# Third attention of a four-layer network: first key and value products split into context and own tokens, part of them moved ahead of the norms

## What is computed

```python
# second feed-forward part, on layernorm(x)
qg, sg = dynamic_quant(x, inv_gate); qu, su = dynamic_quant(x, inv_up)
inter = clip(silu(quant_gemm(qg, sg, w_gate)) * quant_gemm(qu, su, w_up))
x = x + tanh(g) * quant_gemm(*dynamic_quant(inter, inv_inter), w_down)

# third attention, latents = layernorm(x), 32 heads of 128, 4 key/value heads
hidden = concatenate([context, latents], axis=1)      # 64 + 64 tokens per batch
q = latents @ Wq
k, v = hidden @ Wk, hidden @ Wv                       # 4 key/value heads
attn = softmax(q @ k.T / sqrt(128))
x = x + tanh(g) * ((attn @ v) @ Wo)
```

## Time and profile before

| | us |
|---|---|
| median of 3 runs (1638.70 to 1640.34) | 1639.47 |
| the profiled execution's own time | 1636.33 |
| its span, first to last instruction | 1634.5 |
| TensorE busy | 1533.6 (94%) |
| VectorE, ScalarE, GpSimd busy | 905.2, 698.4, 637.8 |
| mean granted TensorE clock | 0.982 of full |

### The profile page before, as it was taken

The page is one execution under the profiler, slowest core; times in us unless marked ns, Lnnn a source line. Parts: engine busy times, 40 slices in busy tenths (PEclk is TensorE's granted clock), DMA queues, the critical chain, the costliest instruction groups (busy, mean ns, idle before and its releaser), DMA issues.

```text
span 1634.5 us, 25536 instructions
## 1 busy us (share of the span) xinstructions
PE 1533.6 (94%) x8786; PEld 1219.5 (75%) x8786; DVE 905.2 (55%) x1805; ACT 698.4 (43%) x2005; POOL 637.8 (39%) x606
## 2 busy tenths in 40 slices
PE   7898989888699999999999998899899999999998
PEld 6666766577588888888888887777677777777776
DVE  7887778768602212222221234687766776676666
ACT  5443244445335435443544445452434343433432
POOL 4643444655413313231322133343644544454430
PEclk9999999899899999999999999899999999999999
DMA  5101110031201000110101011123312212112101
GB/s 213 40 1 39 46 39 1 1 113 46 85 32 40 27 26 27 40 52 2 52 1 52 1 52 58 40 80 83 108 40 78 65 53 73 58 54 76 30 14 53
DMA packets 27885, 81.41 MB, mean 50 GB/s; under 512 B 3248, under 2 KB 11952, under 8 KB 22768
## 3 DMA queue, kind: packets, MB, share of 16 engines
q1 hardware_dynamic: 26896, 79.44, 14.7%
q10 hardware_dynamic: 864, 0.30, 0.1%
HBM read 69.25 MB, written 10.49 MB: 49 GB/s over the span
## 4 chain that ended last, share of the span: by engine, by line
PE 53%; issue 12%; DVE 4%; POOL 3%; ACT 1%; POOLq 0%; DVEq 0%; ACTq 0%
PE bank L397 33%; PE bank L1391 7%; PE bank L1379 2%; PE pair L2453 2%; PE bank L2431 2%; PE pair L1360 2%; POOL wo_low L388 1%; PE pair L397 1%; PE bank L1368 1%; POOL wq_low L1116 1%; PE bank L2439 1%; POOL probs L1125 1%; DVE probs L2285 0%; DVE out_low L2315 0%; DVE small L222 0%
## 5 line engine op out<-in xcount | busy, mean ns | idle before, releaser
L1301 DVE SCALAR_TENSOR_TENSOR x_stream<-bank,gates,x_stream 128x512 f32<-128x512 f32 x64 | 48.1, 751 | 352.3 <-PE bank L1391 352.3
L397 PE MATMUL bank<-hid_high,wq_high 128*128 128x512 f32 (+1 forms) x576 | 234.6, 407 | 1.7 <-issue 1.5
L397 PE MATMUL bank<-hid_high,wq_low 128*128 128x512 f32 (+1 forms) x576 | 220.2, 382 | 0.0
L397 PE MATMUL bank<-hid_low,wq_high 128*128 128x512 f32 (+1 forms) x576 | 218.6, 380 | 0.1
L1125 POOL TENSOR_TENSOR probs<-probs,small 128x512 f32<-128x512 f32 x64 | 67.0, 1048 | 357.5 <-DVE small L1289 357.5
L2180 ACT ACTIVATE probs<-probs,small 128x64 f32<-128x64 f32 x256 | 86.1, 338 | 133.7 <-DVE small L2304 133.7
L397 PEld LDWEIGHTS bank<-hid_high,wq_high 128*128 128x128 f32 x576 | 108.8, 189 | 24.1 <-issue 3.1
L1199 ACT ACTIVATE probs<-pair,small 128x128 f32<-128x128 f32 x256 | 90.5, 366 | 82.6 <-DVE small L1283 82.6
L397 PEld LDWEIGHTS bank<-hid_high,wq_low 128*128 128x128 f32 x576 | 108.7, 189 | 22.6
L397 PEld LDWEIGHTS bank<-hid_low,wq_high 128*128 128x128 f32 x576 | 109.2, 190 | 19.3 <-issue 2.0
L608 POOL TENSOR_TENSOR probs<-probs,small 128x512 f32<-128x512 f32 x64 | 67.2, 1049 | 112.0 <-DVE small L830 111.6
(11 more groups left out here) (382 smaller groups left out, 4185.4 us busy)
## 6 DMA issues: line engine op xcount, KB each, us to landing
raw_q<-in_L_wq SPq DMA_DIRECT2D x18, 1024.0 KB, 4.9
raw_o<-in_L_wo SPq DMA_DIRECT2D x18, 1024.0 KB, 4.9
values<-ctx_values SPq DMA_DIRECT2D x32, 256.0 KB, 3.9
values_t<-ctx_keys SPq DMA_DIRECT2D x8, 512.0 KB, 3.3
raw_c<-in_L_wkv SPq DMA_DIRECT2D x6, 512.0 KB, 3.4
raw_o<-in_L_wkv SPq DMA_DIRECT2D x5, 512.0 KB, 4.6
x_stream<-in_x SPq DMA_DIRECT2D x8, 256.0 KB, 10.7
ctx_keys<-raw_o SPq DMA_DIRECT2D x8, 256.0 KB, 2.0
```

What stands on the lines that cost most here:

```text
L397: last = k.nc.tensor.matmul(out, stationary(a, c), moving(b, c), start=n == 0, stop=n == total - 1)
L1301: nc.vector.scalar_tensor_tensor(xt, k.bank[7][:], gate, xt, ALU.mult, ALU.add).then_inc(k.x_done, 1)
```

## The change

Six things change; what is computed does not.

1. The six products are split by tokens: `wide_context_half(k, e, side)` makes a product over the context tokens (side 0) or the own ones (side 1), 12 matmuls with 256 columns (4 batches by 64 tokens), written with a stride into one half of each batch's columns of the bank. The bank is complete when both have run.
2. The six banks are 0, 1, 4, 5, 6, 7, one per product, and ScalarE evicts each from there.
3. The context halves of e = 0 and 1 run at the end of the integer layer, after `down(7)` and ahead of the barrier; that of e = 2 ahead of the first transposes, those of 3, 4 and 5 between the transposes. The own halves come by group m, once tiles 2m and 2m+1 are in `hid_low`.
4. The split of the first key and value weights moves into slot 11 of the integer layer: the cast on ScalarE ahead of that slot's other work, the subtraction on GpSimd behind the update of tile 6.
5. The three powers of `next_rstd_gpsimd` move from the end of the integer layer into its slots 8, 10 and 12, each ahead of that slot's update.
6. VectorE's norms go by pairs of tiles (apply two, low of the two before), and ScalarE evicts the products between the `hid_high` copies; the four `high_q` come after tile 3.

```diff
+FIRST_BANKS = (0, 1, 4, 5, 6, 7)
+def wide_context_half(k, e, side):
+    m, kv = divmod(e, 2)
+    out = k.bank[FIRST_BANKS[e]][:].rearrange("p (b s n) -> p b s n", b=4, s=2)[:, :, side, :]
+    return product(k, out, lambda s, c: k.wc[s][:, kv * D + c * P:kv * D + (c + 1) * P],
+                   lambda part, c: hid_cols(k, part, c, 4 * m, 4, side), C)
...
@@ attention_middle, gpsimd
-        low_c(0)
         for head in range(4):
             low_q(0, 0, head)
@@ attention_middle, scalar
-        high_c(0)
-        for t in range(T):
+        for t in range(4):
             ln_high_scalar(k, act, t)
-            if t == 2:
-                for head in range(4):
-                    high_q(0, 0, head)
-        for e in range(6):
-            context(0, e)
-            if e in (3, 5):
-                value_back(0, e // 2 - 1, 13 + 2 * (e // 2 - 1))
+        for head in range(4):
+            high_q(0, 0, head)
+        for m in range(3):
+            for e in (2 * m, 2 * m + 1):
+                context(0, e, FIRST_BANKS[e])
+                if m == 2:
+                    value_back(0, e - 4, 13 + 2 * (e - 4))
+            for t in (2 * m + 4, 2 * m + 5):
+                if t < T:
+                    ln_high_scalar(k, act, t)
@@ attention_middle, vector
-        prep_vector(k, dve)
+        for p in range(T // 2 + 1):
+            if p < T // 2:
+                for t in (2 * p, 2 * p + 1):
+                    ln_apply_vector(k, dve, t)
+            if p == 0:
+                last_stats_vector(k, dve)
+            else:
+                for t in (2 * p - 2, 2 * p - 1):
+                    ln_low_vector(k, dve, t)
@@ attention_middle, tensor
-        for t in range(T):
-            ln_transpose_tensor(k, pe, t, k.xn_ready)
-            if t in (3, 5):
-                if t == 3:
-                    pe.wait_ge(k.lo_c, k.at("lo_c", 2))
-                pe.wait_ge(k.xt_lo, k.at("xt_lo", 2))
-                context(0, t // 2 - 1)
-        pe.wait_ge(k.xt_lo, k.at("xt_lo", T))
-        for e in range(2, 6):
-            pe.wait_ge(k.kv_sbuf, k.at("kv_sbuf", e - 1))
-            context(0, e)
-            if e in (3, 5):
-                m = e // 2 - 1
-                values_back(0, m, 13 + 2 * m)
+        def own_tokens(m):
+            pe.wait_ge(k.xt_lo, k.at("xt_lo", 2 * m + 2))
+            for e in (2 * m, 2 * m + 1):
+                wide_context_half(k, e, 1).then_inc(k.kv_psum, 1)
+                if m == 2:
+                    pe.wait_ge(k.xt_lo, k.at("xt_lo", T))
+                    values_back(0, e - 4, 13 + 2 * (e - 4))
+        wide_context_half(k, 2, 0)
+        for p in range(T // 2):
+            for t in (2 * p, 2 * p + 1):
+                ln_transpose_tensor(k, pe, t, k.xn_ready)
+            if p < 2:
+                wide_context_half(k, 3 + p, 0)
+            if p == 1:
+                own_tokens(0)
+                wide_context_half(k, 5, 0)
+            if p >= 2:
+                own_tokens(p - 1)
@@ quant_mlp, gpsimd
+            if s in (8, 10, 12):
+                ln_rstd_gpsimd(k, pool, s // 2 - 4, s // 2 - 2)
             if s >= 5:
                 update(s - 5)
-        next_rstd_gpsimd(k, pool)
+            if s == 11:
+                split_low_gpsimd(k, pool, k.raw_c, k.wc, 1024, k.hi_c, k.at("hi_c", 0), k.lo_c)
@@ quant_mlp, scalar
+            if s == 11:
+                act.wait_ge(k.loaded_c, k.at("loaded_c", 32))
+                act.wait_ge(k.s_psum, k.at("s_psum", T))
+                split_high_scalar(k, act, k.raw_c, k.wc, 1024, k.hi_c)
@@ quant_mlp, tensor
+        pe.wait_ge(k.x_scaled, k.at("x_scaled", T))
+        for e in range(2):
+            pe.wait_ge(k.lo_c, k.at("lo_c", e + 1))
+            wide_context_half(k, e, 0)
```

More of the change, by code:

```diff
@@ L1168, in high_o, with context @@
             split_high_scalar(k, act, k.raw_o, k.wo, 2048, k.hi_o)
-        def context(j, e):
+        def context(j, e, bank=None):
             m = e // 2
@@ L1179, in context @@
                 dst = VT[:, m % 2]
-            nc.scalar.copy(dst, k.bank[4 + e % 2][:]).then_inc(k.kv_sbuf, 1)
+            bank = k.bank[4 + e % 2 if bank is None else bank]
+            nc.scalar.copy(dst, bank[:]).then_inc(k.kv_sbuf, 1)
         def value_back(j, m, s):
```

## The result

| | before | changed |
|---|---|---|
| median, same chip, 4 runs each | 1639.90 | 1627.47 (1626.05 to 1628.89) |
| ratio of the runs, 95% interval | | 0.9928 [0.9916, 0.9940] |
| profiled execution: time, span, clock | 1636.33, 1634.5, 0.982 | 1628.49, 1626.4, 0.983 |
| TensorE busy in it | 1533.6 | 1533.1 |

The gain is 10.9 us**, with an uncertainty of 1.1.

The account below looks back on a forecast made before the run. TensorE, busy 1533.6 of 1634.5 us, was taken as the bound, waiting 8.6 us around the barrier. An earlier release (0.9) and 20.7 instead of 28.35 us to the first query gave 8.5 won: 1631.0 us, range 1628.8 to 1634.0.

Parts of the forecast that it names:

- Barrier: End of the integer layer: sync queue arrives last instead of GpSimd, release at 433.27 against 434.19, 0.9 us won.
- Half products: TensorE around the barrier: matmuls of 256 columns start 0.12 us apart, 1.44 us for each half product of 12.
- The rival of the weight loads: Half-width matmuls go at the weight loads' pace, 0.19 us: 10.1 us more, 1641.1; up to 1654.0 without overlap; chance 0.04.
- Release to first query: TensorE behind the barrier: half products, transposes and waits sum to 20.7 us, against 28.35 before.
- The third tile's wait: Behind the barrier, TensorE waits some 0.7 us for `hid_low` of tile 0 before transposing the third tile.
- ScalarE's cast, GpSimd's subtractions: Ahead of the barrier: cast (1.14 us) and subtractions (2.68 us) fit into idle time; the cast was costed at nothing.
- Clock behind the barrier: TensorE's granted clock is full (PEclk 1.00) from the barrier on, where it was 0.52 before.
- the slow-clock rival: Clock stays low behind the barrier, since TensorE still pauses 0.7 us there: 1632.1 to 1633.8 us; chance 0.16.
- Sum: First query starts at 454.0 instead of 462.54: 8.5 us won in all, barrier included.
- Behind the first query nothing is changed: From the first query on, the third attention's slots should simply come 8.5 us earlier.
- The clock as a constant elsewhere: Outside the edit: 1627.8 from the profiled execution, moved to the median by the same 3.1 us difference, giving 1631.0.
- my own range: Range of the forecast case alone, 1629.8 to 1632.2 us around 1631.0; chance 0.70.

Follow-up runs that it names:

- e8: Changed kernel with the load of raw_o moved from ahead of the barrier to behind it; a single execution gave 1625.62 us.
- e9: Kernel before with only GpSimd's three powers moved, in front of the updates of tiles 4, 5 and 6; 1639.62 us, 0.9999.
- e4: Changed kernel with the context halves of products 0 and 1 put behind the barrier, not ahead of it; 1631.73 us, 0.9947.
- e3: Kernel before with three useless half products added, two ahead of the barrier and one behind it; 1637.24 us, 0.9982.
- e5: Kernel before with 29 long-met waits put between the first query products, moving later TensorE code by 71 instructions; 1638.74 us, 0.9997.
- e12: The same kernel as e5, timed again; 1639.77 us, 0.9996.
- e6: Changed kernel with 75 long-met waits in front of the first queries, its loops placed as in e3 modulo 256 instructions; 1638.39 us, 0.9992.
- e7: Changed kernel with 45 long-met waits in front of the first queries, its loops placed as before modulo 256 instructions; 1630.21 us, 0.9945.
- e11: Changed kernel with GpSimd's three powers put back behind the last update; 1626.75 us, 0.9918.

## Why the prediction was right and wrong

Right, step by step (the profile after against the prediction's terms):

- *Barrier.* Expected: release 0.9 earlier, queue last. Found: the release comes 3.98 us behind the start of the last product (435.06 - 431.08), before 4.82, so 0.84; e8 showed that the queue is last.
- *Half products.* 0.12 a matmul, 1.43 to 1.44 for twelve, as counted. The rival of the weight loads is out. By the Trainium skill (TensorE: Matmul & The Clock Gate, Part 3, The mechanism) a load overlaps only with a matmul in other row groups; the trace disagrees here too, with full rows and a strided output.
- *Release to first query.* Expected 20.7, found 455.55 - 435.06 = 20.49. The third tile's wait 0.49 for 0.7; the waits 0.19 and 0.24 as forecast.
- *ScalarE's cast, GpSimd's subtractions.* Costed at nothing, cost nothing (0.30 and 0.70 left in front of the next instruction).
- *Clock behind the barrier.* Expected 1.00, found 1.00. By the Trainium skill (the same page, Part 4: PE-mode transpose) transposes don't count as work for the clock; that would have been the slow-clock rival, and it did not come.
- *Sum.* 8.5 forecast, 8.7 to 8.9 measured.

Wrong:

- *"Behind the first query nothing is changed."* This step failed. Nothing in the work is changed there, but the edit added instructions to TensorE ahead of two loops, and so moved their code. From the head loop's last product to 189 matmuls on, the two profiles of before took 37.96 and 37.83 us and the three of the change 36.96 to 36.97: **0.9 us** that the sum has no term for (0.5 against e9, 37.49, whose TensorE code is that of before). From the pair loop's last product to 163 on, it was 24.09 and 24.62 before and 23.59, 23.61 and 23.75 in the change, but other kernels with the change's placement and a clock of 1.00 there reach 24.31 (e4), so the 0.7 between the means is not shown to be the change's. The number of added instructions was there to be read, and the 1.09 us at the head loop's jump, of which 0.71 are marked "issue", was in the trace of before; I did not ask what would happen to it.
- *The clock as a constant elsewhere.* I moved the sum from the profiled execution to the median by adding their difference, which is right, and then gave my own range only 1.2 us on both sides, when executions of one kernel spread over 4 us or more for the low clock alone. The four runs of the result, mean clock 0.9848, lie 1.6 us under the mean of 14 (0.9831). That is luck, and without it the time, 1629.1, would lie within 1628.8 to 1634.0. Against it the forecast 1631.0 is still 1.9 us high: the gain is 10.9 for 8.5, of which 0.9 is the head loop, 0.3 the edited stretch (8.8 for 8.5) and 1.2 not assigned, and the median that the forecast started from, 1639.47, lay 0.5 under the mean of before.
What the low clock had cost before, I did not add as a term of its own, and was right not to; e3 puts it at 0.9 us of the stretch, since VectorE's norms set the pace there, and this is contained in the 8.5.

The accounts: 10.9 us (uncertain by 1.1) = 8.8 in the edit + 0.9 at the head loop + 1.2 unassigned, about as much as the uncertainty. That the 0.9 count in full in the time is not shown: e5 and e12 got back only 0.6 of their 2.4 to 2.8.

## What to carry to other kernels

Work that depends on nothing late, moved into the wait at a barrier, is worth what the trace says, and can be summed to some tenths of a microsecond from the durations of before. But ask also where the code of the loops behind it comes to lie: an idle time marked "issue" at a loop's jump back can go or come with an edit ahead of it, and is seen in the number of loads of the instruction queue. And judge edits under 0.2% by the distance between two instructions of the trace, not by the time of the whole, which the low clock moves by more.

## What was not expected of the hardware

- A loop's jump back takes TensorE's time or none by the place of the same code alone: 0.55 to 1.09 or 0.22 from start to start in the head loop; 1.17 to 1.82 or 0.20 in the pair loop.
- Waits that are long met are not always free on TensorE: 75 of them, about 37 instructions, cost 2.9 us in front of the first query in e6, about 0.08 for each instruction, and 1.5 in front of each of the next four; 45 of them cost 1.2 and then nothing (e7).
- Work brought forward into a stretch at the low level gave about a third of its time back: 0.3 of 0.82 us in e9, against 0.85 in e11 with the clock full.
- 3.63 us of idleness in front of dense products left the clock at 1.00 (e4), as 1.65 us did in front of a half product and transposes (e3).
